# Attention with 12 heads on one Trainium2 core: the row maximum enters the second score product through a spare row, and the step lists are reordered

## The chip, the cores and the metric

One core of a Trainium2 chip. The metric is device time in microseconds of one execution of the whole program. The kernel before took 2574.82, 2577.34 and 2578.39 us in three runs, median 2577.34.

## What is computed

32 images of 3x224x224 are cut into 196 patches each and embedded to 192 numbers; 128 text rows are joined, so a batch has T = 324 tokens of D = 192 (three tiles of 108). Then follow a causal attention with rotary positions, and a block with a second attention and a mixture of 8 experts, of which each token takes 2. The change touches the second attention only:

```
qkv = (xn @ qkv_w.T + qkv_b).reshape(Bx, Nx, 3, H, hd).transpose(2, 0, 3, 1, 4)   # H = 12, hd = 16
q, k, v = (qkv[0], qkv[1], qkv[2])
attn = softmax(einsum('bhqd,bhkd->bhqk', q, k) * hd ** -0.5, axis=-1)
o = einsum('bhqk,bhkd->bqhd', attn, v)
```

## The kernel before

**Stages.** The work on a batch is split in a front (embedding, first attention, products for q, k, v of the second), a back (the second attention), a close (projection, norm, gate, places of the tokens, scatter to a buffer in DRAM) and expert tiles of 256 token rows, three a turn. A body of the loop runs the front of batch b, the back of b-1 and the close of b-2. Bodies of the list BOTH also run three expert tiles. The order is: BOTH for batches 0 and 1 (without the parts that have no batch yet), ATTEND for fronts 2 to 18 (17 bodies), BOTH for 19 to 31 (13 bodies), LAST (back of batch 31), CLOSE, and then 17 turns of expert tiles alone (TILES).

**Order by lists.** ATTEND_STEPS, BOTH_STEPS and LAST_STEPS are written out. Each engine runs its own steps in the list's order, and between engines semaphores decide. Each list has its banks of PSUM (..._BANKS): a step on TensorE waits (free) until the step that reads the bank's last contents is done, as FREED says: s is freed by mx, mt by nm, st by ex.

**The second attention, per batch.** A head has 32 partitions, so four heads fill a group g of 128; three groups. 16 rows of a head hold one copy of its 16 numbers, the other 16 a second copy; qm is the f16 part of q in the rows that the mask mq picks, QA = q - qm (L1346), KH = f16(k) (L1027), KL = k - KH (L1348).
- s (L1778, TensorE, 18 steps): the scores of two heads and one tile of queries, two matmuls QA x KH, 32 rows deep, 324 columns. The step's number p even or odd picks partitions 0 to 63 or 64 to 127.
- mx (L1356, VectorE, 18): the row maximum, written in row 0 of each head's 32 in MX, which is otherwise zero.
- mt (L1787, TensorE, 3): three transposes of MX, one group.
- nm (L1042, ScalarE, 3): NM = -MX^T / BIG, f16, from PSUM.
- st (L1801, TensorE, 18): the transposed scores of two heads and one tile of keys, as the sum of three products of two matmuls each: KH x QA, KL x QA, and big16 x NM (big16 is BIG = 32768 everywhere), which subtracts the maximum.
- ex (L1051, ScalarE, 18): the exponential; pv (L1812, TensorE): the product with v; no (L1366 to L1371, VectorE): the division by the sums.

The other steps that the text names: emb (L1657 with tokW, freed by he L1235), tr1 and tr2 (transposes, L1621 and L1622), qk1, v1, qk2, v2, W1, W2, pj, gate (chains, all L1657), s1 (L1728), p1t (L1739), X (L1851) and pos (L1839, L1841) on TensorE; qkh (L1026) and v2e (L1034, L1036) on ScalarE; rm (L1316), m1 (L1325), qkl, the steps of gt1 and pos2 (L1393 to L1440), yv (L1506) on VectorE; scat (L876), ad (L899) and gb (L887) on POOL; xin, keep, lr, lu, ld (loads and stores) on SyncE.

TensorE's steps in a body, in the order of the lists. ATTEND before:

```
s0 s1 s2 emb s3 s4 s5 s6 pj mt0 tr1 s7 st0 st1 st2 s8 qk1.0 qk1.1 s9 st3 v1 s10 st4 st5 s11 s12 s1. s13 mt1 s14 pv0
s15 s16 p1t st6 s17 pv1. st7 mt2 st8 st9 st10 tr3 st11 st12 st13 gate st14 st15 tr2 pv1 pos st16 st17 qk2.0 qk2.1
qk2.2 pv2 v2                                        (s1. and pv1. belong to the first attention)
```

BOTH before:

```
X0 emb s0 s1 W1 pj W1 s2 s3 s4 W1 s5 tr1 W2 s6 s7 W2 s8 s9 qk1.0 X1 v1 W1 s10 s11 qk1.1 mt0 W1 s12 st0 st1 W1 s1. W2
st2 st3 W2 mt1 s13 st4 s14 X2 s15 st5 p1t st6 st7 W1 s16 pv1. tr3 s17 W1 st8 st9 pv0 mt2 W1 st10 st11 gate st12 st13
pv1 W2 st14 pos tr2 st15 W2 st16 st17 qk2.0 qk2.1 pv2 v2 qk2.2
```

## Time and profile before

| | us |
|---|---|
| runs, median | 2577.34 |
| profiled execution | 2573.1 |
| its span, first to last instruction | 2571.3 |
| TensorE (PE) busy | 2368.5 |
| weight loads (PEld), beside PE | 1829.1 |
| VectorE (DVE) busy | 1657.7 |
| ScalarE (ACT) busy | 1156.4 |
| GpSimd (POOL) busy | 1042.0 |

PE is TensorE's matmuls, PEld its weight loads, SP is SyncE, which issues the transfers. Busy times leave out waits. Matmuls are pipelined, so the busy times of neighbouring groups overlap, and the sum over groups is more than the engine's. PEclk is the granted clock of TensorE as a share of 2.4 GHz; it has two levels, 1.2 and 2.4 GHz, so 0.5 is a stretch wholly at the lower. The letter L and a number name a line of the kernel.

### The profile page before, as it was taken

What the parts mean: (1) busy time and instruction counts of PE and PEld (TensorE: products, weight loads), DVE (VectorE), ACT (ScalarE), POOL (GpSimd) and SP (SyncE); (2) the same over time, 40 slices, a digit from 0 to 9 for tenths busy, and PEclk for the clock granted to TensorE, in tenths of its full rate; (3) what the DMA queues carried; (4) which work ended last, traced back from release to release, by engine and by line L of the source; (5) the groups of instructions that cost most, each with busy time, mean ns of one, the idle gap of its engine ahead of it and who ended that gap; (6) DMA issues with size and microseconds to landing.
All of it is one profiled execution on the core that took longest, in us unless ns stands there. A gap on an engine that the chain in (4) does not pass through costs nothing. (4 is left out here: it accounts for less than half of the span.)

```text
span 2571.3 us, 63751 instructions
## 1 busy us (share of the span) xinstructions
PE 2368.5 (92%) x19496; PEld 1829.1 (71%) x19496; DVE 1657.7 (64%) x4146; ACT 1156.4 (45%) x2240; POOL 1042.0 (41%) x1196
## 2 busy tenths in 40 slices
PE   5589999999999999999999999999999987999996
PEld 4456666666666666677777777777777767989886
DVE  3558888888888888867776677766677651111111
ACT  2234444344443344345555555555555643333332
POOL 2103233332333333334444444454444454565565
PEclk7669999999999999899999999999999998999998
DMA  7445222322222322533444554443344355877874
GB/s 135 142 61 111 32 36 35 49 40 32 36 33 44 47 32 32 141 68 102 115 98 106 119 117 104 97 116 91 101 110 106 87 148 183 232 225 225 239 218 132
DMA packets 182885, 268.48 MB, mean 104 GB/s; under 512 B 34085, under 2 KB 150249, under 8 KB 182825
## 3 DMA queue, kind: packets, MB, share of 16 engines
q1 hardware_dynamic: 145960, 235.45, 37.4%
q0 software_dynamic: 36864, 32.27, 7.1%
q8 instruction: 33, 0.54, 0.1%
q14 instruction: 28, 0.22, 0.0%
HBM read 217.71 MB, written 58.33 MB: 107 GB/s over the span
## 5 line engine op out<-in xcount | busy, mean ns | idle before, releaser
L1356 DVE TENSOR_REDUCE MX<-PS 108x2 f32<-108x648 f32 x576 | 455.9, 824 | 46.3 <-PE PS L1778 41.6
L1051 ACT ACTIVATE pool<-PS 108x648 f32<-108x648 f32 x576 | 386.8, 713 | 214.0 <-PE PS L1801 185.7
L899 POOL DMA_INDIRECT out<-big,tokn x192 | 304.2, 1584 | 415.7 <-DVE big L1506 234.0
L1657 PE MATMUL PS<-WB,big 128*128 128x192 f32 x2304 | 405.8, 331 | 2.5 <-ACT big L1080 2.5
L1080 ACT ACTIVATE big<-PS,WF 128x256 f32<-128x256 f32 x576 | 241.9, 473 | 350.3 <-PE PS L1657 348.3
L1657 PEld LDWEIGHTS PS<-WB,big 128*128 128x128 f32 x2304 | 374.8, 191 | 27.8 <-issue 19.1
L1657 PE MATMUL PS<-XE,WF 128*128 128x256 f16 x2880 | 358.9, 276 | 22.8 <-DMA WF<-w1p 15.0
L1657 PEld LDWEIGHTS PS<-XE,WF 128*128 128x128 f16 x2880 | 274.5, 99 | 75.9 <-issue 16.9
L876 POOL DMA_INDIRECT xbuf<-XR,DST x192 | 190.6, 993 | 238.4 <-issue 154.1
L1506 DVE SCALAR_TENSOR_TENSOR big<-PS,grow,GB 128x192 f32<-128x192 f32 x192 | 71.2, 413 | 271.6 <-POOL GB L887 152.7
L1812 PE MATMUL PS<-pool,Vp 108*32 108x324 f32 x2304 | 216.2, 518 | 0.0
L1368 DVE RECIPROCAL rsi<-rsi 128x324 f32<-128x324 f32 x96 | 209.1, 2178 | 3.3
L1778 PE MATMUL PS<-KH,QA 32*108 32x324 f16 x1152 | 155.2, 339 | 48.3 <-DVE MX L1356 11.2
L1657 PE MATMUL PS<-tokW,ximg 96*88 96x192 f32 (+1 forms) x1024 | 196.4, 352 | 3.5 <-issue 2.6
L1657 PEld LDWEIGHTS PS<-tokW,ximg 96*88 96x88 f32 (+1 forms) x1024 | 187.6, 255 | 7.9 <-issue 4.1
L1801 PE MATMUL PS<-QA,KH 32*108 32x324 f16 x1152 | 164.6, 346 | 13.1 <-DVE MX L1356 9.9
L887 POOL TENSOR_SCALAR GB<-WB,grow 128x192 f32<-128x192 f32 x192 | 163.4, 1056 | 29.0 <-DVE grow L1518 24.6
L1778 PEld LDWEIGHTS PS<-KH,QA 32*108 32x108 f16 x1152 | 58.8, 120 | 141.8 <-issue 43.2
L1042 ACT ACTIVATE NM<-PS 128x324 f16<-128x324 f32 x96 | 42.2, 439 | 244.1 <-PE PS L1787 244.1
L1801 PE MATMUL PS<-NM,big 32*108 32x324 f16 x1152 | 150.9, 311 | 0.0
L1801 PE MATMUL PS<-QA,KL 32*108 32x324 f16 x1152 | 150.8, 311 | 0.0
L1812 PEld LDWEIGHTS PS<-pool,Vp 108*32 108x32 f32 x2304 | 73.2, 124 | 99.2 <-issue 58.1
(197 smaller groups left out, 4094.8 us busy)
## 6 DMA issues: line engine op xcount, KB each, us to landing
WF<-w1p SPq DMA_DIRECT2D x96, 771.5 KB, 5.0
WB<-w2p SPq DMA_DIRECT2D x96, 672.0 KB, 6.6
ximg<-in_x SPq DMA_DIRECT2D x96, 196.0 KB, 5.4
XtR<-xbuf SPq DMA_DIRECT2D x96, 196.0 KB, 2.6
ximg<-in_x SPq DMA_DIRECT2D x96, 195.1 KB, 8.7
out<-R SPq DMA_DIRECT2D x32, 243.0 KB
w1p<-WF SPq DMA_DIRECT2D x8, 768.0 KB, 4.1
w2p<-in_L_ffn_W SPq DMA_DIRECT2D x8, 576.0 KB, 8.7
```

The costliest lines, as they stand in the source:

```text
L876: nc.gpsimd.indirect_dma_start(xbuf[:, :], bass.IndirectOffsetOnAxis(ap=DST[:, NT * k + t:NT * k + t + 1], axis=0), XR[:, t, :], None).the ...
L887: last = nc.gpsimd.tensor_scalar(GB[:, i % 2, s_, :], B2t[:, i, :], grow[:, i, s_:s_ + 1], None, ALU.mult)
L899: nc.gpsimd.indirect_dma_start(rows_out, bass.IndirectOffsetOnAxis(ap=tokn[:, i, s_:s_ + 1], axis=0), Yt[:, i, s_, :], None, bounds_check= ...
L1051: nc.scalar.activation(Pr[:, at:at + 2, :], pair(("st", p))[0:TP, :, 0:T], ACT.Exp, scale=SCALE2).then_inc(S["ex"], 1)
L1080: last = nc.scalar.activation(hid[:, i, c, :], ps[:, TILE * (c % 2):TILE * (c % 2) + TILE], ACT.Gelu, bias=WF1[:, i, 2 * HID + c:2 * HID + ...
L1356: nc.vector.tensor_reduce(MX[:, qt, g, 64 * jj:64 * jj + 64:32], pair(("s", p))[0:TP, :, 0:T], AX.X, ALU.max).then_inc(S["mx"], 1)
L1368: nc.vector.reciprocal(at, at).then_inc(S["inv"], 1)
L1506: last = nc.vector.scalar_tensor_tensor(Yt[:, i, s_, :], bank(("W2", i, 0))[:, D * s_:D * s_ + D], grow[:, i, s_:s_ + 1], GB[:, i % 2, s_, ...
L1657: last = nc.tensor.matmul(out_ap, lhsT, rhs, start=(i == 0), stop=(i == len(products) - 1))
L1778: last = nc.tensor.matmul(ps[0:TP, i, 0:T], QA[r, g, TP * qt:TP * qt + TP], KH[r, g, :], start=True, stop=True)
L1801: last = nc.tensor.matmul(ps[0:TP, i, 0:T], left[r], right[r], start=n == 0, stop=n == 2)
L1812: last = nc.tensor.matmul(ps[32 * j:32 * j + 32, 0:T], Vp[:, kt, 4 * g + j, :], Pr[:, at, :], start=kt == 0, stop=kt == NT - 1)
```

## The change

The third product of st goes. The maximum takes a row that the second product has spare: MX is now written from row 16 (HD) of each head on; BIG is added to the bias of that row of k's low part, so that KL holds BIG there (C_TOP, qmb[:, 3:6]); the mask mq now picks rows 0 to 15, so that qm is the f16 part of q there and zero in rows 16 to 31; and nm adds -MX^T / BIG to qm in place, on VectorE instead of ScalarE. st becomes KH x QA + KL x qm: two products, and KL's product with the low part of q is left out. NM and big16 go. All three lists are reordered, with their banks. What is left out of the diff are the hunks of the other lists and banks.

```diff
--- before.py
+++ after.py
@@ -59,7 +59,8 @@
 C_I = C_J + NJ
 C_LE = C_I + NTL
 C_TOK = C_LE + E * E
-C_N = C_TOK + NT
+C_TOP = C_TOK + NT
+C_N = C_TOP + 1
 
 XIN = 6 * 16
 FRONT_STEPS, BACK_STEPS = 6, 17
@@ -83,8 +84,8 @@
     SP=("xin", "text", "keep", "rows0", "rows1", "rows2", "up0", "up1", "up2", "down0", "down1", "down2"),
     PE=("emb", "tr1", "qk1", "v1", "s1", "p1t", "pv1", "tr2", "qk2", "v2", "s", "mt", "st", "pv", "pj", "tr3", "gate",
         "pos", "x_full", "w1", "o_full"),
-    ACT=("tr1h", "v1e", "e1", "p1e", "tr2h", "qkh", "v2e", "nm", "ex", "xm", "xh", "th", "x_evac", "gelu"),
-    DVE=("he", "var0", "n0", "tr1l", "rm", "m1", "rcp", "h1", "var1", "n1", "xf", "tr2l", "qkl", "fstep", "mx", "sums",
+    ACT=("tr1h", "v1e", "e1", "p1e", "tr2h", "qkh", "v2e", "ex", "xm", "xh", "th", "x_evac", "gelu"),
+    DVE=("he", "var0", "n0", "tr1l", "rm", "m1", "rcp", "h1", "var1", "n1", "xf", "tr2l", "qkl", "fstep", "mx", "nm", "sums",
          "inv", "no", "x1", "var3", "na", "n3", "logit", "hot", "tin", "gt2", "pos2", "bstep", "y_done", "gs", "gm"),
     POOL=("eps0", "is0", "rs", "eps1", "is1", "hb", "cx", "ch", "rr", "eps3", "is3", "xl", "gb"))
 
@@ -96,74 +97,74 @@
 ATTEND_STEPS = [
-    ("s", 0), ("text",), ("s", 1), ("s", 2), ("emb",), ("mx", 0), ("s", 3), ("mx", 1), ("mx", 2), ("s", 4), ("he",),
-    ("s", 5), ("mx", 3), ("st0",), ("mx", 4), ("is0",), ("s", 6), ("mx", 5), ("pj",), ("n0",), ("mt", 0), ("tr1",),
-    ("mx", 6), ("x1",), ("nm", 0), ("s", 7), ("st", 0), ("tr1h",), ("st", 1), ("mx", 7), ("st", 2), ("tr1l",),
-    ("ex", 0), ("cx",), ("s", 8), ("mx", 8), ("qk1", 0), ("ex", 1), ("rm", 0), ("qk1", 1), ("ex", 2), ("s", 9),
-    ("st", 3), ("ex", 3), ("v1",), ("rs", 0), ("s", 10), ("rm", 1), ("mx", 9), ("st", 4), ("mx", 10), ("v1e",),
-    ("st", 5), ("ex", 4), ("st3",), ("s", 11), ("ex", 5), ("rs", 1), ("s", 12), ("s1",), ("mx", 11), ("mx", 12),
-    ("s", 13), ("mt", 1), ("m1",), ("s", 14), ("is3",), ("mx", 13), ("pv", 0), ("e1",), ("mx", 14), ("s", 15),
-    ("mx", 15), ("s", 16), ("p1t",), ("nm", 1), ("mx", 16), ("st", 6), ("n3",), ("p1e",), ("s", 17), ("ex", 6),
-    ("pv1",), ("st", 7), ("ex", 7), ("mx", 17), ("xin",), ("rcp",), ("mt", 2), ("nm", 2), ("st", 8), ("h1",),
-    ("st1",), ("is1",), ("st", 9), ("ex", 8), ("st", 10), ("tr3",), ("ex", 9), ("st", 11), ("no", 0), ("ex", 10),
-    ("xm",), ("st", 12), ("ex", 11), ("st", 13), ("n1",), ("xh",), ("ex", 12), ("gate",), ("ex", 13), ("st", 14),
-    ("st", 15), ("tr2",), ("tr2h",), ("gt1",), ("rr",), ("tr2l",), ("pv", 1), ("pos",), ("ex", 14), ("st", 16),
-    ("st", 17), ("ex", 15), ("pos2",), ("ex", 16), ("qk2", 0), ("ex", 17), ("keep",), ("ch",), ("qk2", 1), ("qkh", 0),
-    ("th",), ("xl",), ("no", 1), ("qkl", 0), ("qkh", 1), ("gt2",), ("qk2", 2), ("pv", 2), ("v2",), ("qkl", 1),
-    ("hb",), ("qkh", 2), ("qkl", 2), ("xf",), ("no", 2), ("v2e",), ("scat",),
+    ("s", 0), ("text",), ("emb",), ("mx", 0), ("s", 1), ("s", 2), ("he",), ("mx", 1), ("s", 3), ("st0",), ("mx", 2),
+    ("mx", 3), ("is0",), ("s", 4), ("pj",), ("n0",), ("tr1",), ("mx", 4), ("xin",), ("tr1h",), ("x1",), ("s", 5),
+    ("mx", 5), ("rr",), ("tr1l",), ("s", 6), ("mx", 6), ("s", 7), ("mt", 0), ("nm", 0), ("qk1", 0), ("st", 0),
+    ("mx", 7), ("rm", 0), ("qk1", 1), ("rm", 1), ("s", 8), ("st", 1), ("ex", 0), ("v1",), ("s", 9), ("rs", 0),
+    ("ex", 1), ("mx", 8), ("v1e",), ("s", 10), ("s", 11), ("rs", 1), ("mx", 9), ("s", 12), ("mx", 10), ("st", 2),
+    ("s1",), ("mx", 11), ("st3",), ("st", 3), ("mx", 12), ("m1",), ("st", 4), ("ex", 2), ("s", 13), ("ex", 3),
+    ("s", 14), ("mx", 13), ("mx", 14), ("mt", 1), ("keep",), ("ex", 4), ("e1",), ("s", 15), ("nm", 1), ("st", 5),
+    ("ex", 5), ("ch",), ("s", 16), ("cx",), ("mx", 15), ("p1t",), ("mx", 16), ("is3",), ("s", 17), ("n3",), ("rcp",),
+    ("p1e",), ("st", 6), ("ex", 6), ("st", 7), ("pv1",), ("mx", 17), ("h1",), ("mt", 2), ("ex", 7), ("st", 8),
+    ("nm", 2), ("st", 9), ("pv", 0), ("tr3",), ("ex", 8), ("ex", 9), ("st1",), ("st", 10), ("xm",), ("st", 11),
+    ("ex", 10), ("xh",), ("ex", 11), ("st", 12), ("st", 13), ("gate",), ("st", 14), ("ex", 12), ("ex", 13), ("is1",),
+    ("st", 15), ("no", 0), ("n1",), ("tr2",), ("pv", 1), ("gt1",), ("tr2h",), ("xl",), ("hb",), ("pos",), ("ex", 14),
+    ("tr2l",), ("ex", 15), ("st", 16), ("th",), ("pos2",), ("st", 17), ("gt2",), ("v2",), ("ex", 16), ("qk2", 0),
+    ("ex", 17), ("no", 1), ("scat",), ("pv", 2), ("qkh", 0), ("qk2", 1), ("xf",), ("qkl", 0), ("v2e",), ("qk2", 2),
+    ("no", 2), ("qkh", 1), ("qkl", 1), ("qkh", 2), ("qkl", 2),
 ]
...
@@ -362,17 +363,16 @@
         nw = sb("nw", [128, 2], F32)
         n2 = sb("n2", [TP, 2, D], F32)
         qkb = sb("qkb", [128, 6], F32)
-        qmb = sb("qmb", [128, 3], F32)
+        qmb = sb("qmb", [128, 6], F32)
         cst = sb("cst", [128, C_N], F32)
         ident = cst[:, C_ID:C_ID + 128]
-        m64, mq = (cst[:, c:c + 1] for c in (C_M64, C_MQ))
+        m64, mq, top = (cst[:, c:c + 1] for c in (C_M64, C_MQ, C_TOP))
         rev = cst[0:TP, C_REV:C_REV + NT * E].rearrange("p (t e) -> p t e", t=NT)
         id16 = sb("id16", [128, 128], F16)
         idb = sb("idb", [TP, TP], BF16)
         maskb = sb("maskb", [TP, TP], BF16)
         U16 = sb("U16", [TP, TP], F16)
         ones16 = sb("ones16", [TP, TP], F16)
-        big16 = sb("big16", [128, TP], F16)
 
         ximg = sb("ximg", [128, GRID * IMG], F32)
         H = sb("H", [TP, NT, D], F32)
@@ -401,7 +401,6 @@
         X1 = sb("X1", [TP, NT, D], F32)
         NB = sb("NB", [TP, NT, D], F32)
         MX = sb("MX", [TP, NT, NG3, 128], F32)
-        NM = sb("NM", [128, NG3, T], F16)
         pool1 = sb("pool1", [128, 18 * T], F32)
         Pr = pool1[0:TP, :].rearrange("p (i t) -> p i t", t=T)
         tokD = pool1[0:96, 768 * 4:768 * 5].rearrange("p (s n m) -> p s n m", s=2, n=4)
@@ -777,7 +776,6 @@
             nc.gpsimd.memset(big[0:96, 2688:3456], 0.0).then_inc(pad_set, 1)
             nc.gpsimd.memset(Vp[:, :, :, :], 1.0).then_inc(pad_set, 1)
             nc.gpsimd.memset(MX[:, :, :, :], 0.0).then_inc(pad_set, 1)
-            nc.gpsimd.memset(big16[:, :], BIG).then_inc(pad_set, 1)
             nc.gpsimd.memset(zrow[:, :, :], 0.0).then_inc(zero_set, 1)
             pool.wait_ge(zero_set, 1)
             nc.gpsimd.memset(zrow[:, :, D:D + 1], NOWHERE).then_inc(zero_set, 1)
@@ -1036,11 +1034,6 @@
                 nc.scalar.activation(Vp[:, 2, :, 0:HD], ps[0:TP, 1, 0:D].rearrange("p (h d) -> p h d", h=HEADS),
                                      ACT.Copy).then_inc(S["v2e"], 1)
 
-            def nm(b, g):
-                act.wait_ge(S["mt"], due("mt", b, g + 1))
-                act.wait_ge(S["st"], due("st", b - 1, 6 * g + 6))
-                nc.scalar.activation(NM[:, g, :], bank(("mt", g))[:, 0:T], ACT.Copy, scale=-1.0 / BIG).then_inc(S["nm"], 1)
-
             def ex(b, p):
                 act.wait_ge(S["st"], due("st", b, p + 1))
                 if p >= 9:
@@ -1092,7 +1085,7 @@
                         attention_weights()
                         continue
                     if kind == "preps":
-                        act.wait_ge(pad_set, 4)
+                        act.wait_ge(pad_set, 3)
                         prep("qkv")
                         continue
                     if kind == "ready":
@@ -1116,8 +1109,6 @@
                         qkh(b, step[1])
                     elif kind == "v2e":
                         v2e(b)
-                    elif kind == "nm":
-                        nm(b, step[1])
                     elif kind == "ex":
                         ex(b, step[1])
                     elif kind == "xm":
@@ -1196,7 +1187,8 @@
 
             def query_bias():
                 dve.wait_ge(qb_in, 128)
-                nc.vector.tensor_scalar(qmb[:, :], qkb[:, 0:3], mq, None, ALU.mult).then_inc(bias_ready, 1)
+                nc.vector.tensor_scalar(qmb[:, 0:3], qkb[:, 0:3], mq, None, ALU.mult)
+                nc.vector.tensor_scalar(qmb[:, 3:6], qkb[:, 3:6], top, None, ALU.add).then_inc(bias_ready, 1)
 
             def attention_weights():
                 for i, (v, hi, lo) in enumerate(early):
@@ -1345,7 +1337,7 @@
                 ps = pair(("qk2", j))
                 nc.vector.scalar_tensor_tensor(QA[:, j, :], ps[:, 0, 0:T], qkb[:, j:j + 1], qm[:, j, :],
                                                ALU.add, ALU.subtract)
-                nc.vector.scalar_tensor_tensor(KL[:, j, :], ps[:, 1, 0:T], qkb[:, 3 + j:4 + j], KH[:, j, :],
+                nc.vector.scalar_tensor_tensor(KL[:, j, :], ps[:, 1, 0:T], qmb[:, 3 + j:4 + j], KH[:, j, :],
                                                ALU.add, ALU.subtract).then_inc(S["qkl"], 1)
 
             def mx(b, p):
@@ -1353,8 +1345,13 @@
                 dve.wait_ge(S["s"], due("s", b, p + 1))
                 if p % 6 == 0:
                     dve.wait_ge(S["mt"], due("mt", b - 1, g + 1))
-                nc.vector.tensor_reduce(MX[:, qt, g, 64 * jj:64 * jj + 64:32], pair(("s", p))[0:TP, :, 0:T], AX.X,
+                nc.vector.tensor_reduce(MX[:, qt, g, 64 * jj + HD:64 * jj + 64:32], pair(("s", p))[0:TP, :, 0:T], AX.X,
                                         ALU.max).then_inc(S["mx"], 1)
+
+            def nm(b, g):
+                dve.wait_ge(S["mt"], due("mt", b, g + 1))
+                nc.vector.scalar_tensor_tensor(qm[:, g, :], bank(("mt", g))[:, 0:T], -1.0 / BIG, qm[:, g, :],
+                                               ALU.mult, ALU.add).then_inc(S["nm"], 1)
 
             def no(b, g):
                 dve.wait_ge(S["pv"], due("pv", b, g + 1))
@@ -1570,6 +1567,8 @@
                         qkl(b, step[1])
                     elif kind == "mx":
                         mx(b, step[1])
+                    elif kind == "nm":
+                        nm(b, step[1])
                     elif kind == "no":
                         no(b, step[1])
                     elif kind == "x1":
@@ -1794,11 +1793,10 @@
                 free(pe, turn, ("st", p))
                 ps = pair(("st", p))
                 k = slice(TP * kt, TP * kt + TP)
-                for n, (left, right) in enumerate(((KH[:, g, k], QA[:, g, :]), (KL[:, g, k], QA[:, g, :]),
-                                                   (big16[:, :], NM[:, g, :]))):
+                for n, (left, right) in enumerate(((KH[:, g, k], QA[:, g, :]), (KL[:, g, k], qm[:, g, :]))):
                     for i in range(2):
                         r = slice(64 * jj + 32 * i, 64 * jj + 32 * i + 32)
-                        last = nc.tensor.matmul(ps[0:TP, i, 0:T], left[r], right[r], start=n == 0, stop=n == 2)
+                        last = nc.tensor.matmul(ps[0:TP, i, 0:T], left[r], right[r], start=n == 0, stop=n == 1)
                 last.then_inc(S["st"], 1)
 
             def pv(turn, b, g):
@@ -1887,7 +1885,7 @@
                         continue
                     if kind == "preps":
                         pe.wait_ge(act_const, 1)
-                        pe.wait_ge(pad_set, 4)
+                        pe.wait_ge(pad_set, 3)
                         pe.wait_ge(zero_set, 3)
                         pe.wait_ge(qkv_in, 16)
                         prep("qkv")
@@ -1988,7 +1986,8 @@
     p = np.arange(128)
     c[:, C_ID:C_ID + 128] = np.eye(128, dtype=np.float32)
     c[:, C_M64] = p >= 64
-    c[:, C_MQ] = p % 32 >= HD
+    c[:, C_MQ] = p % 32 < HD
+    c[:, C_TOP] = np.where(p % 32 == HD, BIG, 0.0)
     j = np.arange(RH, dtype=np.float32)
     theta = np.power(np.float32(10000.0), np.float32(-2.0) * j / np.float32(D), dtype=np.float32)
     ang = np.arange(T, dtype=np.float32)[None, :] * theta[:, None]
@@ -2007,7 +2006,7 @@
     c[:, C_J:C_J + NJ] = np.arange(NJ) * TILE
     c[:, C_I:C_I + NTL] = np.arange(NTL)
     e = np.arange(E)
-    c[0:TP, C_TOK:C_N] = np.arange(TP)[:, None] + TP * np.arange(NT)[None, :]
+    c[0:TP, C_TOK:C_TOP] = np.arange(TP)[:, None] + TP * np.arange(NT)[None, :]
     c[:, C_LE:C_TOK] = (e[None, :] <= e[:, None]).reshape(-1)
     return c
```

TensorE's steps after, in the same manner. ATTEND:

```
s0 emb s1 s2 s3 s4 pj tr1 s5 s6 s7 mt0 qk1.0 st0 qk1.1 s8 st1 v1 s9 s10 s11 s12 st2 s1. st3 st4 s13 s14 mt1 s15 st5 s16
p1t s17 st6 st7 pv1. mt2 st8 st9 pv0 tr3 st10 st11 st12 st13 gate st14 st15 tr2 pv1 pos st16 st17 v2 qk2.0 pv2 qk2.1 qk2.2
```

BOTH:

```
X0 emb W1 s0 s1 pj W1 s2 s3 s4 W1 s5 tr1 s6 s7 W2 s8 s9 W2 s10 s11 qk1.0 X1 qk1.1 W1 v1 s12 s13 W1 mt0 s14 s15 W1 st0
st1 s1. W2 st2 st3 W2 st4 st5 mt1 X2 p1t st6 st7 W1 s16 pv1. s17 tr3 W1 mt2 st8 st9 pv0 W1 st10 st11 gate st12 st13 pv1
W2 st14 tr2 st15 W2 st16 st17 qk2.0 qk2.1 pos pv2 v2 qk2.2
```

The image load xin stands 31st of 200 steps in BOTH instead of 147th, and 19th of 149 in ATTEND instead of 87th.

## Rows read from the trace of the kernel before

**Rows 1.** The page: busy time of each engine, and the span in 40 slices

```profile
PE 2368.5 (92%) x19496; PEld 1829.1 (71%) x19496; DVE 1657.7 (64%) x4146; ACT 1156.4 (45%) x2240; POOL 1042.0 (41%) x1196
...
PE   5589999999999999999999999999999987999996
```

**Rows 2.** Windows: stretch, its us, busy us by engine, PEclk, DMA share, GB/s

```profile
185.02:1053.54 868.52, 811.03 (x6848) 570.48 (x6846) 760.93 (x1810) 355.32 (x720) 290.96 (x384) 0.94 0.27 44
1113.82:1973.82 860.00, 849.99 (x7296) 657.13 (x7296) 607.26 (x1524) 484.44 (x865) 386.11 (x432) 0.98 0.47 107
...
2130.00:2571.30 441.30, 393.24 (x3067) 367.48 (x3065) 66.46 (x274) 159.15 (x357) 244.32 (x210) 0.96 0.72 208
...
1401.05:1472.88 71.83, 70.98 (x609) 54.76 (x609) 50.61 (x128) 40.26 (x72) 32.17 (x36) 0.98 0.47 107
1472.88:1543.06 70.18, 69.33 (x609) 54.27 (x610) 50.55 (x128) 40.27 (x72) 32.16 (x36) 1.00 0.47 108
...
101.77:185.02 83.25, 64.97 (x400) 41.71 (x400) 47.27 (x84) 25.34 (x47) 9.62 (x13) 0.67 0.36 83
```

**Rows 3.** Line L1235 (he), 32 instructions, one for each batch

```profile
L1235 DVE TENSOR_TENSOR H<-PS,tokb x32: 345/358/359, 27.7 to 1973.8; 108x192 f32<-108x192 f32 x32
```

**Rows 4.** Waits in 185 to 1054 us: who waited for whom, us, times, longest

```profile
PEld PS L1778 <- DVE MX L1356: 23.9, 50, 3.8
PEld PS L1801 <- DVE MX L1356: 20.9, 48, 0.6
...
DVE H L1235 <- PE PS L1657: 23.2, 16, 5.5
DVE posn L1427 <- PE PS L1841: 19.7, 16, 1.8
DVE tmp L1316 <- PE PS L1657: 14.6, 16, 0.9
```

**Rows 5.** Groups by form, whole span: count, busy us, mean ns, idle before

```profile
L1801 PE MATMUL PS<-NM,big 32*108 32x324 f16 x1152 | 150.9, 311 | 0.0
...
L1348 DVE SCALAR_TENSOR_TENSOR KL<-PS,qkb,KH 128x324 f16<-128x324 f32 x96 | 52.4, 546 | 0.0
...
L1042 ACT ACTIVATE NM<-PS 128x324 f16<-128x324 f32 x96 | 42.2, 439 | 244.1 <-PE PS L1787 244.1
```

**Rows 6.** Timeline: start us, us, engine; a lone st, a pair of st, qkl

```profile
748.58 0.34 PE L1801 MATMUL PS<-QA,KH 32*108 32x324 f16 x2
748.76 0.30 PE L1801 MATMUL PS<-QA,KL 32*108 32x324 f16 x2
748.89 0.30 PE L1801 MATMUL PS<-NM,big 32*108 32x324 f16 x2
749.12 0.50 PE L1787 MATMUL PS<-cst,MX 108*128 108x108 f32 x3
...
599.90 0.45 PE L1801 MATMUL PS<-QA,KH 32*108 32x324 f16 x4
600.08 0.41 PE L1801 MATMUL PS<-QA,KL 32*108 32x324 f16 x4
600.22 0.41 PE L1801 MATMUL PS<-NM,big 32*108 32x324 f16 x4
600.59 0.58 PE L1657 MATMUL PS<-XT,qkvWa 128*128 128x324 f16 x3
...
712.21 0.55 DVE L1346 SCALAR_TENSOR_TENSOR QA<-PS,qkb,qm 128x324 f16<-128x324 f32 x1
712.67 0.55 DVE L1348 SCALAR_TENSOR_TENSOR KL<-PS,qkb,KH 128x324 f16<-128x324 f32 x1
```

**Rows 7.** Windows of 3 us, columns as in rows 2: two BOTH bodies, an ATTEND body

```profile
1449.00:1452.00 3.00, 3.00 (x27) 0.99 (x25) 2.23 (x13) 2.97 (x5) 0.34 (x1) 0.59 0.66 272
...
1521.00:1524.00 3.00, 3.00 (x31) 2.19 (x24) 2.57 (x14) 2.97 (x5) 0.17 (x1) 1.00 0.51 212
...
758.00:761.00 3.00, 3.00 (x25) 0.99 (x24) 2.15 (x10) 1.46 (x3) 0.00 (x0) 0.50 0.00 0
```

1 line of the change is left out of this document (added), and 141 rows, old and new, of tables (ATTEND_BANKS, BOTH_BANKS, BOTH_STEPS, LAST_BANKS).

## The prediction

> **What bounds the kernel now.** I read the page first for shares, then cut the span into its stages. TensorE is busy 2368.5 us of 2571.3, VectorE 1657.7, ScalarE 1156.4 [rows 1]; the slices show three regimes. The windows by stage [rows 2] run between first additions of he (L1235), which each attention body has once [rows 3]. 185 to 1054 us holds 16 rounds of the ATTEND body, 54.28 us each: TensorE busy 811.03 of 868.52 (93.4%), VectorE 760.93 (87.6%). 1114 to 1974 holds 12 BOTH bodies, 71.67 each: TensorE 849.99 of 860.00 (98.8%), VectorE 607.26 (70.6%). Then come the rest of the last BOTH body, LAST and CLOSE, and from about 2130 the expert tiles alone, 441 us, which hold no step that the change touches. So TensorE sets the pace of BOTH by itself. In ATTEND it leads too, with VectorE close behind.
>
> Who waits for whom in ATTEND [rows 4]: TensorE's weight loads wait for the row maxima (MX L1356) before s and st, for 0.5 us at a time; all its idle time, 868.52 less 811.03 [rows 2], is 57.5 us, 3.6 a body. VectorE idles 107.6 us, 6.7 a body, and its three longest waits, all for TensorE (L1657, L1841), are 57.5 us of that, 3.6 a body; what is left, 3.1, is shorter waits and its own chains.
>
> **The change part by part.**
>
> *The third product.* 1152 matmuls out<-NM,big go, two for each of 576 st steps. Their row says 150.9 us busy [rows 5], but busy time overlaps with the neighbours and is not the price. The price is read from starts [rows 6]. A lone st begins its three products at 748.58, 748.76 and 748.89 and the next step starts at 749.12: a product of two matmuls takes one slot of 0.13 to 0.14 us. Two st steps side by side, whose heads lie in different halves of the partitions (0 to 63, 64 to 127), start their products at 599.90, 600.08 and 600.22 as fours and are through at 600.59: 0.69 us for two, against 0.54 for one. So a neighbour is almost free, and a removed product of a full pair is worth one slot for both.
> The Trainium skill (TensorE: Matmul & The Clock Gate, the section Why this matters for your kernels) says that small-K matmuls in distinct row groups run concurrently. By that rule alone, with all steps in pairs, the product is worth 9 slots a body, half of 18. The starts agree for real pairs, but the lists don't pair every step.
> So I count slots from the lists: in each unbroken run of s and st steps on TensorE, one slot for each s, three (after: two) for each st, separately for even and odd heads' halves, and the larger sum counts. ATTEND goes from 47 to 32 slots, BOTH from 45 to 31, LAST from 43 to 36. That takes in the new order as well. At 0.137 us: 2.05 us a body in ATTEND, 1.9 in BOTH, 1.0 in LAST. Bounds: 9 slots (1.2 us), if only full pairs had counted, and 18 (2.5 us), if no pair overlapped.
>
> *nm moves from ScalarE to VectorE.* ScalarE loses 96 activations of 439 ns [rows 5], 1.3 us a body. It is busy 355 of 868 us in ATTEND and 484 of 860 in BOTH [rows 2]: worth nothing by itself. VectorE gets 96 operations on 128x324, PSUM f32 with an f16 operand to f16. The nearest row is KL (L1348), the same shape, operation and kinds: 546 ns mean, 52.4 us in all. Starts inside a burst are 0.46 us apart (QA at 712.21, KL at 712.67) [rows 6]. I take 0.55, so 1.65 us a body; bounds 0.46 and 0.65, for a wait for mt at each. Being in order, VectorE stands at nm until mt's three transposes are through, and mx, m1, x1 and the others stand behind it; who waits for those is TensorE, at the next s for a free bank. The lists put steps between mt and st (qk1 in ATTEND, s and W1 in BOTH), so st itself is covered there.
> In BOTH VectorE goes from 50.6 to 52.3 us of 71.7: hidden. In ATTEND it goes from 47.6 to 49.2, while TensorE goes from 50.7 to 48.7. The two are level. Of the 3.1 us of VectorE's idle time that is no long wait I count half, 1.5, as chains that stay, so a body can hardly be under 50.7 by VectorE. TensorE needs 48.7 and some of the 3.6 us of its waits, which grow as VectorE is later in relation to it. I let 1.3 of the 2.05 us through: body 53.0. Bounds: a gain of 2.5, if all slots count and the waits stay, and a loss of 1.65, if VectorE's whole idle time stays and the new operations lengthen the body.
>
> *The small ones.* MX in row 16 of a head's 32, qm and QA with halves exchanged, BIG added to KL's bias: same instructions, same shapes, 0. NM and big16 go, one memset less on POOL at the start, one tensor_scalar on 128x3 more, both behind the input loads: 0, bounds -0.5 and 0.5. qkh still waits for the st steps of the batch before: 0. The result loses the product of the two low parts, which is no time. The other moved steps (xin, keep, lr, lu, ld on SyncE's queue, scat, ad, gb on POOL's) issue the same transfers. POOL is busy 291 of 868 us and 386 of 860, the DMA share is 0.27 and 0.47 [rows 2]; I take 0, within the ends already given. The image load xin now stands early in both bodies instead of late.
>
> *The ends.* Body 1, before 185 us, has the first back part: TensorE 64.97 us busy of 83.25 at a clock of 0.67 [rows 2]. 14 slots at half clock are 3.8 us; with so much idle time I take 2, bounds 0 and 4. LAST: 1, bounds 0 and 2. Expert tiles: 0.
>
> *Sum.* 17 ATTEND bodies (batches 2 to 18) x 1.3 = 22; 13 BOTH bodies x 1.9 = 25; 2 + 1. Together 50 us. The profiled execution took 2573.1 (span 2571.3), so 2523; the median shown is 2577.3, 4.2 above it, so **2527**. Ends: gains of 17 x 2.5 + 13 x 2.5 + 6 = 81 give 2496; 17 x 1.65 lost, 13 x 1.2 won give 2590.
>
> **The clock** is the term that no row can fix. Two BOTH bodies with the same instructions took 71.83 and 70.18 us [rows 2]. In the first, a stretch shows a granted clock of 0.59, in the other it is 1.00 at the same place [rows 7]: one stretch at 1.2 instead of 2.4 GHz costs 1.65 us. It stands behind the gate products (8 columns each) and the st steps and the pv that follow, not behind idle time: TensorE is busy 3.00 of 3.00 us there, and so it is in ATTEND (758 to 761, at 0.50). The change takes matmuls out of just this part.
> The same page of the Trainium skill (the section HAM oscillation) blames gaps in which TensorE idles for the return to the low clock. By that rule the change would cost nothing here, as it makes no long gap. The trace differs: the drops come with TensorE busy, so the rule takes no risk off the sum.
>
> **The rivals.**
> *A, VectorE takes over ATTEND.* The three nm's wait for mt and stand in front of maxima; TensorE's faster steps only wait longer. ATTEND gains nothing, BOTH its 25: 2573.1 - 28 + 4.2 = 2549. For it: 87.6% before, and the MX waits. Against: 3.6 us a body of VectorE's idle time is long waits for TensorE, twice the 1.65 added.
> *B, the slots all count.* TensorE passes on everything at the upper ends: 2496 + 4 = 2500. For it: BOTH has no slack; unequal neighbours overlap poorly. Against: ATTEND's second engine is near.
> *C, slower: more half-clock stretches.* From one more stretch in each of 30 bodies (30 x 1.65 = 50 us) the gain is gone. Two more in each ATTEND body and one in each BOTH body are 47 x 1.65 = 78 us: 2573.1 - 50 + 78 + 4.2 = 2605. For it: less work on TensorE in the part where the clock already falls. Against: the gate, pv, pos and transposes in that part stay as they are, and the bodies shorten anyhow.
> *D, the change doesn't do what it says,* because the lists let the products go where TensorE was waiting. In BOTH, with 1.2% idle, that can't be; in ATTEND it is rival A. TensorE at its old pace in BOTH too would give 2577, with next to no chance.
>
> **How the numbers follow.** The forecast with its neighbourhood (2510 to 2542) 0.50; A 0.20; B 0.15; C 0.10; D beyond A, and what lies between no gain and the worst sum, 0.05. A measurement here tells about 0.2%, 5 us, from no change. Faster: forecast, B, nearly all of A and a little of the rest, 0.85. C and the worst sum give 0.10 slower, 0.05 same. The range holds B's centre and A with a clock stretch in half of the bodies: 2494 to 2568.
>
> **What would show it.** Right: L1801 has four matmuls a step (2304, not 3456); BOTH bodies about 69.8 us with TensorE still over 97% busy; ATTEND bodies about 53 us with VectorE at 92 to 93% and TensorE near it; the new VectorE rows near 0.55 us; the expert tiles unchanged at 441. A: ATTEND stays at 54 us, and TensorE waits for L1356 more than now. B: ATTEND under 52 us. C: a mean granted clock under the present 0.94 and 0.98 in these stages. The forecast is wrong if BOTH gains under 1 us a body, or if the gain comes from the expert tiles.

## The result, and the profile after

The change makes the kernel slower: 2714.23 us, median of four runs (2710.8 to 2720.45), against 2576.08 of the kernel before in the same comparison. The ratio is 1.056 [1.0535, 1.0585]. The forecast was 2527; its range, 2494 to 2568, doesn't hold the result. The profiled execution took 2711.8 us, its span is 2710.0, 138.7 above that of before. Medians here and in the table of the experiments are over all runs of a kernel; one run of e2 and two of e5 lie more than 1.5% above that kernel's fastest, and without them the medians are 2697 and 2814 us.

The page of the kernel after: span, TensorE's busy time, and two rows of the 40 slices (compare [rows 1]; before, the digits of PEclk were 9 from the fourth slice on but for three).

```profile
span 2710.0 us, 61359 instructions
...
PE 2424.8 (89%) x18344; PEld 1839.5 (68%) x18344; DVE 1711.0 (63%) x4243; ACT 1122.5 (41%) x2144; POOL 1043.6 (39%) x1195
...
PE   4589999998999999989999999999999986999996
...
PEclk8668787788778787789999999999999998999998
```

TensorE has 1152 matmuls less and is busy 56 us longer. The digits 7 and 8 of PEclk from the fourth slice to the eighteenth, which hold the ATTEND bodies, are what is new. The windows by stage (columns as in [rows 2]) give the sizes: start, 16 ATTEND bodies, 12 BOTH bodies, the last expert tiles.

```profile
101.77:190.35 88.58, 65.44 (x374) 40.73 (x372) 47.30 (x85) 24.14 (x44) 9.93 (x13) 0.67 0.32 78
190.35:1161.56 971.21, 889.44 (x6272) 601.68 (x6270) 774.44 (x1859) 344.25 (x672) 290.09 (x384) 0.81 0.25 39
...
1225.56:2102.17 876.61, 829.46 (x6864) 641.18 (x6862) 637.63 (x1560) 466.25 (x829) 383.95 (x427) 0.97 0.46 104
2268.00:2710.00 442.00, 392.33 (x3054) 367.17 (x3054) 65.90 (x271) 158.50 (x357) 241.73 (x207) 0.96 0.72 206
```

An ATTEND body takes 971.21 / 16 = 60.70 us instead of 54.28, 102.7 us in all; a BOTH body 73.05 instead of 71.67, 16.6 us in all. The start before the first of these bodies costs 5.3 us, the ATTEND body between the two stages 3.7, and what follows the last addition of he 10.3; the expert tiles are as before (442 us). Granted clock in ATTEND: 0.81 instead of 0.94. Time at half clock is twice the missing share: 2 x 0.19 x 971.21 = 369 us after, 2 x 0.06 x 868.52 = 104 us before. The unrounded clock record of the traces says 373 and 97; further such times in this text are from that record, between the first and the last addition of he of the 16 bodies. (The texts on the runs, written before them, name the same times up to 3 us higher, as 375 and 232 for 373 and 229.)

Three rows of the groups by form (columns as in [rows 5]): the two products that are left, and nm in its new place.

```profile
L1799 PE MATMUL PS<-QA,KH 32*108 32x324 f16 x1152 | 153.8, 379 | 21.3 <-DVE Os L1368 7.0 <-ACT XM L1050 4.9 <-DVE qm L1353 3.0
L1799 PE MATMUL PS<-qm,KL 32*108 32x324 f16 x1152 | 139.8, 339 | 0.0
...
L1353 DVE SCALAR_TENSOR_TENSOR qm<-PS,qm 128x324 f16<-128x324 f32 x96 | 46.5, 484 | 4.1 <-PE PS L1786 3.9
```

The product is gone, and nm takes 484 ns, where 550 was forecast.

**Where the clock falls.** Windows of 3 us in the ATTEND body from 369.70 to 428.66, in two stretches:

```profile
387.00:390.00 3.00, 2.27 (x20) 1.33 (x17) 2.67 (x9) 1.05 (x2) 1.06 (x2) 1.00 0.00 0
390.00:393.00 3.00, 2.76 (x25) 1.47 (x23) 3.00 (x6) 2.49 (x9) 0.00 (x0) 0.96 0.00 0
393.00:396.00 3.00, 3.00 (x14) 2.39 (x12) 2.75 (x8) 1.70 (x3) 0.00 (x0) 0.50 0.00 0
...
405.00:408.00 3.00, 2.40 (x21) 2.05 (x21) 2.76 (x11) 0.68 (x2) 1.01 (x2) 0.73 0.00 0
408.00:411.00 3.00, 3.00 (x23) 1.12 (x26) 1.90 (x9) 1.46 (x3) 0.00 (x0) 0.50 0.00 0
```

And TensorE's timeline through the first fall (start, us, engine, line, operation, out<-in):

```profile
390.74 0.34 PE L1777 MATMUL PS<-KH,QA 32*108 32x324 f16 x2
391.14 0.34 PE L1799 MATMUL PS<-QA,KH 32*108 32x324 f16 x2
...
391.88 0.76 PE L1738 MATMUL PS<-cst,P 108*108 108x108 f32 x6
...
393.02 0.51 PE L1799 MATMUL PS<-QA,KH 32*108 32x324 f16 x2
393.32 0.48 PE L1799 MATMUL PS<-qm,KL 32*108 32x324 f16 x2
393.78 4.17 PE L1656 MATMUL PS<-V,P1T 108*108 108x192 f32 x12
```

From 388.35 to 393.78 TensorE runs only 32-row products (s, st) and transposes (mt, p1t), with gaps of 0.73 and 0.18 us. Inside this run, at 392.73 by the clock record, the lower level is granted and everything takes longer: a lone product's row goes from 0.34 to 0.51 us, and the twelve matmuls of pv1 behind it take 4.17 us. The second fall (406.39) stands behind the gate, as it did before [rows 7]. In the old list pv0, 24 matmuls over 108 partitions, stood inside the first of these runs; the new list has it behind mt2, st8 and st9.

The clock record of all 16 bodies shows that this body is one of four of its kind. In the other twelve the lower level comes earlier, 16 to 19 us behind the addition of he, when TensorE has run s9 to s12 and st2 and is at s1. of the first attention; that is ahead of the place that pv0 had. Of the 373 us at half clock, 27 belong to the fall at 23 us that is shown here, 174 to the earlier one, 31 to another in nine bodies (8 us behind the addition of he, behind tr1, s5 to s7 and mt0), and 140 to the one behind the gate, where the kernel before had nearly all of its 97. So the place of pv0 can explain the new falls of this kernel in part only.

Are the gaps the cause? In BOTH before, the stretches ahead of the fall of [rows 7] have none:

```profile
1443.00:1446.00 3.00, 3.00 (x39) 2.00 (x33) 1.67 (x3) 2.58 (x4) 2.77 (x6) 1.00 1.16 116
1446.00:1449.00 3.00, 3.00 (x36) 2.16 (x34) 2.93 (x7) 2.77 (x4) 3.00 (x5) 0.84 1.07 242
```

The fall itself begins at 1448.06, and the pv that the prediction counts to its causes starts only at 1448.95. Ahead of all eleven falls of these 12 bodies TensorE is busy without a gap for 6 us (by the profile, which models the ends of matmuls). So a fall needs no idle time there that the profile shows. In the last 2.5 us ahead of 1448.06 TensorE ran st and the gate's products, and before them the wide products of a W1. That thin work alone (few rows, or few columns) is enough is what this suggests; in ATTEND thin work and gaps stand together, and the runs below separate them only in part.

**Where BOTH loses.** Two waits that the trace of before doesn't have among its long ones, from the waits of 1225.56 to 2102.17, and VectorE's and POOL's timeline at the start of one body:

```profile
DVE Nrm L1262 <- POOL rsf L811: 32.3, 11, 3.0
PE PS L1777 <- DVE X L1378: 31.3, 11, 2.9
```

```profile
1736.78 0.98 POOL L874 DMA_INDIRECT xbuf<-XR,DST  x1 [0.30 <-issue]
1737.90 1.51 POOL L885 TENSOR_SCALAR GB<-WB,grow 128x192 f32<-128x192 f32 x2
...
1739.66 0.90 POOL L811 TENSOR_TENSOR rsf<-vef,cst 108x3 f32<-108x3 f32 x1
1740.68 0.96 DVE L1262 TENSOR_SCALAR Nrm<-H,mvf,rsf 108x192 f32<-108x192 f32 x3 [2.95 <-POOL rsf L811]
...
1742.52 0.34 PE L1777 MATMUL PS<-KH,QA 32*108 32x324 f16 x2 [2.86 <-DVE X L1378]
```

The new list ends a body with scat and begins the next with gb0 ahead of is0, all on POOL: scat's transfers are still being issued until 1737.8, gb0 takes 1.5 us, is0 comes behind it, and VectorE stands at n0 with x1 and the maxima behind it. TensorE waits 2.9 us for them in this body, 31.3 in 12.

### The profile page after: what moved, and what is told of

It is laid out like the page before. It is cut to its first block and busy times, and to the rows that moved or that the text cites. A ratio compares the mean times of both kernels' runs of the same rounds, so it can differ in the third digit from the quotient of the medians.

```text
span 2710.0 us, 61359 instructions
## 1 busy us (share of the span) xinstructions
PE 2424.8 (89%) x18344; PEld 1839.5 (68%) x18344; DVE 1711.0 (63%) x4243; ACT 1122.5 (41%) x2144; POOL 1043.6 (39%) x1195
## 5 line engine op out<-in xcount | busy, mean ns | idle before, releaser
L1656 PE MATMUL PS<-WB,big 128*128 128x192 f32 x2304 | 412.6, 335 | 3.5 <-ACT big L1073 3.5
L1656 PEld LDWEIGHTS PS<-WB,big 128*128 128x128 f32 x2304 | 381.1, 194 | 25.9 <-issue 16.1
L1777 PE MATMUL PS<-KH,QA 32*108 32x324 f16 x1152 | 168.2, 363 | 79.5 <-DVE X L1378 33.9
L1810 PE MATMUL PS<-pool,Vp 108*32 108x324 f32 x2304 | 209.6, 504 | 1.7 <-ACT pool L1044 1.7
L885 POOL TENSOR_SCALAR GB<-WB,grow 128x192 f32<-128x192 f32 x192 | 170.5, 1130 | 76.0 <-DVE grow L1515 74.4
L1799 PE MATMUL PS<-QA,KH 32*108 32x324 f16 x1152 | 153.8, 379 | 21.3 <-DVE Os L1368 7.0
L833 POOL TENSOR_TENSOR tmp<-tmp 96x324 f32<-96x324 f32 x64 | 55.4, 866 | 274.4 <-DVE tmp L1308 274.4
L816 POOL TENSOR_TENSOR vef<-mvf,cst 108x3 f32<-108x3 f32 x32 | 6.8, 212 | 353.1 <-DVE mvf L1236 353.1
L1799 PE MATMUL PS<-qm,KL 32*108 32x324 f16 x1152 | 139.8, 339 | 0.0
```

Of the source, the lines that this page charges most:

```text
L885: last = nc.gpsimd.tensor_scalar(GB[:, i % 2, s_, :], B2t[:, i, :], grow[:, i, s_:s_ + 1], None, ALU.mult)
L1656: last = nc.tensor.matmul(out_ap, lhsT, rhs, start=(i == 0), stop=(i == len(products) - 1))
L1777: last = nc.tensor.matmul(ps[0:TP, i, 0:T], QA[r, g, TP * qt:TP * qt + TP], KH[r, g, :], start=True, stop=True)
L1799: last = nc.tensor.matmul(ps[0:TP, i, 0:T], left[r], right[r], start=n == 0, stop=n == 1)
L1810: last = nc.tensor.matmul(ps[32 * j:32 * j + 32, 0:T], Vp[:, kt, 4 * g + j, :], Pr[:, at, :], start=kt == 0, stop=kt == NT - 1)
```

## The experiments

Times are medians; ratios are to the kernel before, measured beside it on the same chip, with the 95% interval. The median of the kernel before was 2576 us beside after, 2579 beside e1 to e4, 2585 beside e5 to e8, 2582 beside e9 and e10, 2589 beside e11 and e12, and 2592 beside e13 to e16. So between these groups ratios are to be compared, not times, and a body's mean carries the same uncertainty, up to 0.6%. "Body" is the mean of the 16 ATTEND and the 12 BOTH bodies, "half" the time at half clock in the 16 ATTEND bodies.

| kernel | us | ratio | ATTEND body | half | BOTH body |
|---|---|---|---|---|---|
| before | 2576 | 1 | 54.28 | 97 | 71.67 |
| after | 2714 | 1.056 [1.0535, 1.0585] | 60.70 | 373 | 73.05 |
| e1 content, old lists | 2649 | 1.0267 [1.0235, 1.0299] | 58.72 | 229 | 71.74 |
| e2 old content, new lists | 2700 | 1.0468 [1.0442, 1.0494] | 58.38 | 227 | 74.97 |
| e3 after, third product of zeros | 2690 | 1.0445 [1.0424, 1.0467] | 57.84 | 201 | 74.26 |
| e4 after, nm on ScalarE | 2716 | 1.0551 [1.0522, 1.0579] | 60.08 | 336 | 74.56 |
| e5 after, wide filler | 2839 | 1.0983 [1.0925, 1.104] | 65.41 | 189 | 73.77 |
| e6 after, thin filler | 2780 | 1.0761 [1.0739, 1.0783] | 64.52 | 324 | 72.46 |
| e7 before, 9 wide at the gate | 2587 | 1.0007 [0.9989, 1.0025] | 54.93 | 34 | 71.74 |
| e8 after, gb0 behind n0 | 2712 | 1.0494 [1.0462, 1.0526] | 61.09 | 305 | 72.30 |
| e9 e1, third product of zeros | 2648 | 1.0261 [1.0235, 1.0287] | 58.27 | 185 | 71.64 |
| e10 before, 3 wide at the gate | 2558 | 0.9914 [0.9894, 0.9934] | 53.65 | 44 | 71.66 |
| e11 two products, nm on ScalarE | 2682 | 1.0355 [1.0323, 1.0387] | 60.22 | 246 | 71.69 |
| e12 e11, 3 wide at the gate | 2645 | 1.0212 [1.0187, 1.0236] | 58.93 | 192 | 71.40 |
| e13 after, pv0 earlier | 2744 | 1.0569 [1.0516, 1.0621] | 62.37 | 257 | 73.08 |
| e14 after, 3 wide at the gate | 2738 | 1.0551 [1.0519, 1.0583] | 62.26 | 373 | 72.96 |
| e15 e13 and e14 | 2745 | 1.0592 [1.0555, 1.0629] | 62.59 | 281 | 73.35 |
| e16 e1, 3 wide at the gate | 2675 | 1.0343 [1.0291, 1.0395] | 59.20 | 208 | 71.62 |

**Content and lists apart (e1, e2).** e1 is the kernel after with the three lists and the banks of before; e2 is the kernel before with those of after. The head of e1's diff against after:

```diff
 ATTEND_STEPS = [
-    ("s", 0), ("text",), ("emb",), ("mx", 0), ("s", 1), ("s", 2), ("he",), ("mx", 1), ("s", 3), ("st0",), ("mx", 2),
+    ("s", 0), ("text",), ("s", 1), ("s", 2), ("emb",), ("mx", 0), ("s", 3), ("mx", 1), ("mx", 2), ("s", 4), ("he",),
...
```

> The change's two products and nm on VectorE, in the lists and banks of the kernel before. Theory L (the order of the lists makes the clock fall more often): the ATTEND body stays near 54.3 us or gains up to 2, half-clock time between 180 and 1110 us stays near 113 us, total 2530 to 2570. Rival W (it is the missing work of the third product that lets the clock fall, wherever it stood): total above 2640, half-clock time there above 250 us. Rival V (nm on VectorE holds up the chain, the clock follows): above 2600, with VectorE waiting for L1786 and TensorE for VectorE at st.

> The new lists and banks with the old three products and nm on ScalarE. Theory L: slow by itself, above 2640, half-clock time in ATTEND above 250 us. Rival W: near the kernel before, 2560 to 2600, with the ATTEND body at 54 to 56 us. Rival V: the same as W.

Each half loses alone, 70 and 121 us, and together 138, less than the sum. Theory L fell with e1, and rivals W and V, both of which had e2 near the kernel before, fell with e2; what each said of the other run came out in part only (for e1 V's waits did show, and 229 us at half clock is under W's 250; for e2 227 us is under L's 250). The windows of e2, of ATTEND and of BOTH:

```profile
189.19:1123.26 934.07, 857.17 (x6848) 599.21 (x6846) 759.70 (x1810) 364.36 (x720) 290.55 (x384) 0.88 0.26 41
1186.30:2085.97 899.67, 850.17 (x7296) 658.01 (x7294) 628.68 (x1525) 478.87 (x865) 386.15 (x427) 0.97 0.45 102
```

In BOTH the two can be read one by one: the lists cost 3.3 us a body (71.67 to 74.97; the wait behind POOL above is 2.6 to 2.9 of it in the kernel after), the content on these lists gives 1.9 back (74.97 to 73.05), just the forecast size; on the old lists it gives nothing (71.74). In ATTEND both lower the clock. The windows of e1, of ATTEND and of BOTH, and rows of its waits in ATTEND:

```profile
184.47:1123.94 939.47, 836.51 (x6272) 574.43 (x6270) 778.43 (x1858) 343.69 (x672) 291.09 (x384) 0.88 0.25 41
1187.43:2048.36 860.93, 831.54 (x6864) 634.58 (x6864) 621.03 (x1561) 469.66 (x829) 386.57 (x432) 0.98 0.47 106
```

```profile
DVE qm L1353 <- PE PS L1786: 23.4, 16, 3.3
...
PE PS L1799 <- DVE H L1331: 19.4, 16, 1.2
...
PE PS L1777 <- DVE qm L1353: 11.6, 16, 0.7
PE PS L1799 <- DVE qm L1353: 11.4, 16, 0.8
```

In BOTH TensorE is idle 860.93 - 831.54 = 29.4 us where it was idle 10.0: what the slots give becomes waits. In ATTEND VectorE stands at nm for the transposes, and TensorE waits behind it at s and st (L1331 is h1, which stands right behind the last nm on VectorE). These three waits of TensorE are 42.4 us, 2.65 a body, more than the 2.05 that the slots were to give.

**The missing product back (e3, e9).** A third product with zeros, which adds nothing to the sum, on the new lists (e3) and on the old (e9).

```diff
-((KH[:, g, k], QA[:, g, :]), (KL[:, g, k], qm[:, g, :]))
+((KH[:, g, k], QA[:, g, :]), (KL[:, g, k], qm[:, g, :]), (KL[:, g, k], zed[:, :]))
```

> The kernel after with a third product KL x zeros in each st, which adds nothing to the scores and waits for nothing new. Theory L: as slow as the kernel after or slower by its 15 to 18 slots, 2710 to 2760. Rival W: the clock comes back, 2560 to 2620, so more work is less time. Rival V: 2710 to 2760.

> Old lists, the change's content (nm on VectorE, maximum in the second product), and a third product KL x zeros in each st: against the kernel before only nm's engine and its place differ, against the content on old lists only the third product is back. Theory W alone: half-clock time in ATTEND back from 232 us to 95 to 120, body 54 to 55, total 2565 to 2595. Rival G (on the old lists it is the gaps that nm on VectorE opens ahead of st and s that let the clock fall, not the missing work): half-clock time stays above 180 us, body 58 or more, total above 2640. Both in part: between.

On the new lists 1152 more matmuls make the kernel 24 us faster (30 us by the ratios): half-clock time goes from 373 to 201 us. That lies between the theories, none of which it fits: W wanted 2620 at most, L and V 2710 at least. On the old lists they change nothing (2649, 2648), and rival G comes out in all its signs. e9 does as many matmuls as the kernel before, and only nm's engine and place (and the operands of the third product) differ; it takes 66 us more and stands 185 us at half clock instead of 97:

```profile
183.38:1115.68 932.30, 844.51 (x6848) 599.27 (x6846) 773.75 (x1858) 344.84 (x672) 291.41 (x384) 0.90 0.24 41
```

So on the old lists nm on VectorE costs by itself nearly all that the whole content costs. TensorE waits there as in e1, 40.8 us for nm and for the h1 behind it, and is idle 87.8 us instead of 57.5. The bodies of e3 are of two kinds by turns, all of the same instructions:

```profile
357.66:412.80 55.14, 50.63 (x430) 35.33 (x428) 48.11 (x115) 21.56 (x42) 18.16 (x24) 0.94 0.25 37
412.80:473.71 60.91, 56.56 (x430) 39.42 (x428) 48.20 (x115) 21.55 (x42) 18.14 (x24) 0.83 0.20 34
```

TensorE is busy 5.9 us longer in the second at the same idle time, 4.4 to 4.5 us: the whole difference is the clock. At half clock it spends 6.8 and 20.5 us, so one us there costs 0.42 us.

**Who does nm (e4, e11, e12).** In e4 nm goes back to ScalarE, which writes -MX^T / BIG to a tile that nothing reads: the maximum isn't subtracted, and the exponent's scale is divided by 64 so that it stays finite. e11 computes all of it without that: old lists, two products, and mt itself adds qm, by one 128-row matmul per group, so that ScalarE can write the sum. e12 adds e10's filler to it.

```diff
 # e4, on ScalarE
+nc.scalar.activation(NM[:, g, :], bank(("mt", g))[:, 0:T], ACT.Copy, scale=-1.0 / BIG)
 # e11, in mt on TensorE, and on ScalarE; idn is -BIG on the diagonal
+nc.tensor.matmul(ps[:, 0:T], idn[:, :], qm[:, g, :], start=True, stop=False)
+nc.scalar.activation(qm[:, g, :], bank(("mt", g))[:, 0:T], ACT.Copy, scale=-1.0 / BIG)
```

> The kernel after with nm back on ScalarE into NM, which no product reads: the maximum is not subtracted, and the exponent's scale is cut to a 64th. VectorE has its old load. Rival V: the loss goes, below 2620. Theories L and W: within 20 us of the kernel after, 2690 to 2720.

> Old lists; the change's two products and layout, but nm stays on ScalarE: mt adds to its transposes one 128-row product of qm with -32768 times the identity in the same bank, and nm writes -1/32768 of the bank over qm. Against the kernel before 18 narrow products go, three wide ones come, VectorE has its old load. Theory G (on the old lists the content's loss is nm on VectorE): no gaps ahead of st, BOTH body 69.5 to 70.5 us, ATTEND 52.5 to 54.5, half-clock time in ATTEND under 130 us, total 2535 to 2570. Rival W (missing work of the third product lets the clock fall): half-clock time above 200 us, ATTEND 56 or more, total above 2600.

> The kernel above with the three wide matmuls ahead of the gate chains of ATTEND bodies, which gained 24 us on the kernel before. If the two gains add: 2515 to 2545, the best of all. If the clock falls elsewhere now: no better than the kernel above.

e4 is as slow as after: with the new lists nm's engine is not the cause, as L and W said and V didn't. e11 has no wait for VectorE's nm and still loses 93 us: G falls here, and W's signs all come (246 us at half clock, a body of 60.22, 2682 us). So on the old lists the loss comes with nm on VectorE and all products (e9), and it comes with nm on ScalarE and two products (e11); neither is needed for it. e11 isn't clean, though: its mt has three 128-row matmuls more, and its transposes add to them. Two bodies of e11, one behind the other:

```profile
419.88:475.18 55.30, 50.21 (x406) 35.75 (x404) 47.33 (x113) 22.35 (x45) 18.20 (x24) 0.94 0.25 37
475.18:542.68 67.50, 58.70 (x406) 39.57 (x404) 47.61 (x113) 22.35 (x45) 18.22 (x24) 0.80 0.20 30
```

12.2 us apart with the same instructions; 8.5 us of it is longer busy time, 3.7 are waits that come with it. With e12's filler half-clock time goes from 246 to 192 us and 37 us come back, more than the 24 that it gave on the kernel before, though far from the 2515 to 2545 that were named if the gains add.

**Wide or thin (e5, e6).** One matmul of zeros more behind each s and st of ATTEND, 36 a body, over 128 rows in e5 and over 32 in e6; it adds nothing to the sums.

```diff
+if turn.plan is ATTEND:
+    r = slice(0, 128)                          # e6: slice(64 * jj + 32, 64 * jj + 64)
+    last = nc.tensor.matmul(ps[0:TP, 1, 0:T], zed[r, :], qkvWa[r, 0, 0:T], start=False, stop=True)
```

> The kernel after, and behind each s and each st of ATTEND bodies one more matmul of 324 columns over all 128 rows, zeros times a weight tile, added to the second bank: 36 slots, 4.9 us of new TensorE work a body, nothing waits for more. Theory W (the clock falls because stretches of 32-row products and transposes keep too few rows of the array at work): half-clock time in ATTEND falls from 23.5 us a body to under 8, the body from 60.7 to 53 to 57 us, total 2590 to 2660. Rival I (the clock falls for TensorE's idle gaps, or for the lists as such): half-clock time stays, the body is 60.7 + 4.9, total 2760 to 2800.

> The same, but each filler has 32 rows instead of 128, in the same row group as the step's second head: the same number of instructions and columns, a quarter of the rows. Theory W: the half-clock time stays above 15 us a body, the body 60 to 65 us, total at least 60 us above the wide filler's. Rival I or a rival by which any instruction counts alike: within 20 us of the wide filler.

```profile
186.52:1233.01 1046.49, 984.88 (x6852) 638.23 (x6852) 782.45 (x1859) 349.10 (x672) 290.82 (x384) 0.91 0.23 36
```

```profile
188.39:1220.68 1032.29, 919.93 (x6848) 630.84 (x6847) 779.35 (x1858) 341.37 (x672) 290.15 (x384) 0.84 0.23 37
```

The same number of matmuls: the wide ones (first fence, e5) bring half-clock time from 373 to 189 us, the thin ones (second fence, e6) to 324. So it goes with the rows more than with the number of matmuls. But neither is free: both kernels are slower than after, and no time came back; W had e5 at 2590 to 2660 and e6 at least 60 us above it, and e6 is below it. Bodies of e5 with 3.4 us at half clock take 61.0 to 62.4 us, one of e8 with as much (below) 54.7: the 36 wide fillers cost 6.3 us or more, 0.18 each at the least. Idle time fell too in e5 (61.6 us against 81.8) and rose in e6 (112.4), so the two causes aren't wholly apart here.

**Wide work at the gate (e7, e10).** The kernel before with 128-row matmuls of 324 columns ahead of each of the gate's three chains, nine a body in e7, three in e10. They write columns of the gate's bank that nothing reads.

```diff
 for t in range(NT):
     c = slice(TP * t, TP * t + TP)
+    if turn.plan is ATTEND:
+        for _ in range(1):                     # e7: range(3)
+            nc.tensor.matmul(ps[0:TP, 64:64 + T], id16[:, 0:TP], qkvWa[:, 0, 0:T], start=True, stop=True)
```

> The kernel before, and ahead of each of the three gate chains of an ATTEND body three 128-row matmuls of 324 columns into unused columns of gate's bank: 9 slots, 1.2 us. Theory W: the half-clock stretch behind the gate (6.2 us a body, worth 3 us) goes or shrinks; ATTEND body 52.3 to 53.5 us against 54.3, total 2545 to 2565. Rival I: body 55.5, total 2595 to 2600.

> The kernel before with one 128-row matmul of 324 columns ahead of each gate chain of an ATTEND body, three in place of the nine of the run above. If the clock needs only a little more work there: half-clock time in ATTEND under 60 us at a third of the cost, body 53.3 to 54.0, total 10 to 20 us below the kernel before. If it needs all nine: half-clock time stays near 99 us, and the body is longer by 0.4 to 0.8 us, total 5 to 15 us above.

The windows of ATTEND in e7 (first fence) and in e10:

```profile
182.09:1060.98 878.89, 806.62 (x6992) 581.89 (x6990) 758.45 (x1811) 355.78 (x720) 291.28 (x384) 0.98 0.26 43
```

```profile
180.93:1039.27 858.34, 794.35 (x6896) 564.78 (x6894) 760.27 (x1810) 355.81 (x720) 291.69 (x384) 0.97 0.27 45
```

Three are the better trade: clock 0.97 instead of 0.94, TensorE busy 794.35 us instead of 811.03 [rows 2] with 48 more matmuls, and 2557.72 us, 0.9914 [0.9894, 0.9934] of before. It is the fastest version of the study. Nine raise the clock to 0.98, with 34 us at half clock, as expected, but cost as much as that gives: 2587 us, where 2545 to 2565 were expected.

**POOL's order in BOTH (e8).** The kernel after with gb0 behind n0 instead of ahead of s0.

```diff
-    ("X", 0), ("text",), ("xe", 0), ("emb",), ("gm", 0), ("W1", 0, 0), ("he",), ("gb", 0), ("s", 0), ("s", 1),
-    ("st0",), ("pj",), ("mx", 0), ("mx", 1), ("ge", 0, 0), ("is0",), ("n0",), ("W1", 0, 1), ("x1",), ("s", 2),
+    ("X", 0), ("text",), ("xe", 0), ("emb",), ("gm", 0), ("W1", 0, 0), ("he",), ("s", 0), ("s", 1),
+    ("st0",), ("pj",), ("mx", 0), ("mx", 1), ("ge", 0, 0), ("is0",), ("n0",), ("gb", 0), ("W1", 0, 1), ("x1",), ("s", 2),
```

> The kernel after with one step of the BOTH list moved: gb of tile 0 stands behind n0 instead of ahead of s 0. Theory P (in BOTH the new list makes POOL, still busy with scat and then gb, late for is0, so that n0 and x1 on VectorE and the next s on TensorE wait): BOTH body shorter by 1.0 to 1.6 us, total 13 to 21 us below the kernel after. Rival (the wait for x1 has another cause): no difference.

TensorE's longest wait for X falls from 2.9 to 1.4 us, and a BOTH body from 73.05 to 72.30 us, 9 us in 12, less than the 1.0 to 1.6 us a body that were expected:

```profile
PE PS L1777 <- DVE X L1378: 13.0, 11, 1.4
```

So gb0 is part of that wait; that scat's issues are the rest is argued from the timeline above, not tried. The ratio fell from 1.056 to 1.0494, but the profiled spans are level (2709.8 and 2710.0), since the 16 ATTEND bodies, which the edit doesn't touch, went from 60.70 to 61.09, and the one behind them from 64.0 to 67.1. They show how far the clock moves them with the waits that come with it (one of the two shortest, and the longest):

```profile
442.15:496.90 54.75, 48.14 (x394) 32.53 (x392) 48.16 (x115) 21.29 (x42) 18.18 (x24) 0.97 0.26 38
...
251.21:319.34 68.13, 59.40 (x394) 40.06 (x392) 48.39 (x115) 21.44 (x42) 18.16 (x24) 0.75 0.20 30
```

The rows stand here in the order of their length. 13.4 us lie between them, at 3.4 and 34.1 us of half clock: 0.44 us for one us.

**Two of the places at which after's clock falls (e13 to e16).** e13 is after with pv0 back in the first run of thin steps, behind s17; e14 is after with e10's three matmuls at the gate; e15 has both; e16 is e1 with those three.

```diff
-    ("ex", 5), ("ch",), ("s", 16), ("cx",), ("mx", 15), ("p1t",), ("mx", 16), ("is3",), ("s", 17), ("n3",), ("rcp",),
+    ("ex", 5), ("ch",), ("s", 16), ("cx",), ("mx", 15), ("p1t",), ("mx", 16), ("is3",), ("s", 17), ("pv", 0), ("n3",), ("rcp",),
...
-    ("nm", 2), ("st", 9), ("pv", 0), ("tr3",), ("ex", 8), ("ex", 9), ("st1",), ("st", 10), ("xm",), ("st", 11),
+    ("nm", 2), ("st", 9), ("tr3",), ("ex", 8), ("ex", 9), ("st1",), ("st", 10), ("xm",), ("st", 11),
```

> The kernel after, with one step moved in the ATTEND list on TensorE: pv0 (matmuls over 108 partitions) goes from behind mt2, st8, st9 to behind s17, into the stretch of s, mt, st, s, p1t behind which the granted clock of after falls first in a body (0.50 at 393 to 399 us). Theory 1, what matters is wide work between the thin steps: the first fall goes in most ATTEND bodies, half-clock time in the 16 bodies goes from 375 us to under 250, the ATTEND body from 60.7 to 57.5 us or less, about 2660 us in all. Theory 2, the fall doesn't depend on this place (another step is late, or the clock falls whenever the body is this short): half-clock time stays over 320 us and the time within 2700 to 2725.

> The kernel after with three added 128-row, 324-column matmuls at the gate of each ATTEND body (their results go to columns of the gate bank that nothing reads), the edit that took 24 us off the kernel before. Theory 1: it guards the second stretch only (the gate), so half-clock time goes from 375 to between 200 and 300 us and the time to 2660 to 2690. Theory 2, the same edit is worth as much as before or less, because the bodies only settle in another pattern: half-clock time over 320 us, 2700 or more.

> Both edits: pv0 earlier and three 128-row matmuls at the gate in ATTEND. Theory 1, the clock is the whole of the ATTEND loss and these two stretches are where it falls: half-clock time under 120 us, the ATTEND body 54 us or less, 2590 to 2620 us in all (what is left over the kernel before is the reordered lists' wait in BOTH and the start). Theory 2, more than these stretches count: half-clock time 200 us or more, time over 2640.

> The content of the change on the old lists (two products, maximum merged on VectorE), with three added 128-row matmuls at the gate of each ATTEND body. Theory 1, the 70 us that the content cost on the old lists are clock: half-clock time in ATTEND from 232 us to under 120, the body from 58.7 to about 54.5, time 2580 to 2600. Theory 2, they are waits of TensorE for VectorE, and the clock follows them: half-clock time stays over 180, time 2635 or more.

The theory that the two guarded places bring the time back fell: e14, e15 and e16 came out as the second theory of each said. e13 is split: half-clock time falls from 373 to 257 us, nearly as the first said, but the time doesn't fall (ratio 1.0569, after 1.056), as the second said. With pv0 moved, the falls 8 us behind the addition of he go from nine bodies to two, and the long ones at 16 to 19 us from twelve to three; the other thirteen bodies keep 6.8 us at 24.5 us and 6.8 us behind the gate. But the moved pv0 waits for the read of its bank by a maximum:

```profile
PE PS L1810 <- DVE MX L1348: 44.9, 16, 3.0
```

2.8 us a body, and the rest of the body shifts with it. Twelve of its bodies take 61.4 to 61.5 us each, with 13.7 us at half clock each:

```profile
565.02:626.43 61.41, 51.19 (x394) 34.08 (x392) 47.82 (x116) 21.25 (x42) 18.09 (x24) 0.89 0.23 34
626.43:687.87 61.44, 51.19 (x394) 34.04 (x392) 47.81 (x116) 21.25 (x42) 18.09 (x24) 0.89 0.22 34
```

TensorE is idle 10.2 us in such a body, twice as long as in one of after, and stands less at half clock: the falls don't follow idle time alone. In e14 the filler at the gate changed nothing (373 us; ratio 1.0551 against 1.056), and in e16 it changed a body that varied (57 to 64 us) into one of 58.0 us, thirteen times, with half-clock time at 208 instead of 229 us; the ratio rose from 1.0267 to 1.0343. What the filler gave before (24 us) and in e12 (37 us) it doesn't give here. So guarding a place doesn't tell by itself what comes of it: the falls at other places move or stay, and the bodies settle in a pattern that repeats, a good or a bad one. That a fall makes what follows late and so moves the next thin run is the likely link; no run shows it alone.

## Why the prediction was wrong

**The step that failed is the term of the clock.** The text named it "the term that no row can fix", saw the falls in the part from which matmuls were to be taken, had rival C for it, and then left it out of the sum with a chance of 0.10. C's size was also too small: two stretches more in each ATTEND body and 78 us; measured are 276 us more at half clock in 16 bodies, 17.2 us in each, and at 0.35 to 0.44 us for one us (after's own bodies, 58.8 us with 17.1 and 62.4 with 27.3, and e8's) this is 97 to 121 us of the 102.7.

The sum for an ATTEND body closes with it. Slots: -2.05, as forecast. Idle time of TensorE: 81.8 us instead of 57.5, +1.5. Clock: 276 x 0.4 / 16 = +6.9 (0.4 taken between the two). Together +6.4; measured +6.42. For a BOTH body: slots -1.9; idle time 47.2 us in 12 instead of 10.0 in 12, +3.1; clock 48 against 38 us, +0.3; together +1.5; measured +1.4. In BOTH, e2 against after measures the slots together with nm's move: 1.9. In ATTEND the -2.05 is not measured: with 0.35 to 0.43 for the clock the sum leaves room for 1.1 to 2.5. Bodies with near the same time at half clock give a rough size: with 20.5 us TensorE is busy 56.5 us in e3 and 55.7 in e2, which have the third product, and 54.6 in after (between its bodies with 17.1 and 23.9 us, 53.6 and 55.6). So the product was worth 1.1 to 1.9 us of busy time there, under the 2.05 of the forecast.

**C's argument against itself failed.** "The gate, pv, pos and transposes in that part stay as they are, and the bodies shorten anyhow." They stayed, but new falls came in other places: 232 of the 373 us don't lie behind the gate. The list moved pv0 out of the first thin run, and in e2, with the same list, 15 of the 16 bodies fall there, 6.8 us each; in after four do, and twelve fall earlier, for which no run isolates a cause. I counted slots in the new lists and didn't read them for the runs between wide steps. e2 shows what that was worth: the lists alone, with all three products, bring half-clock time from 97 to 227 us. The content alone brings it to 229 (e1), nm on VectorE with all products to 185 (e9), and two products with nm on ScalarE, and mt changed for it, to 246 (e11).

**Moved steps on POOL at 0 was wrong** in BOTH: the new order costs 3.3 us a body, most of it the wait behind scat at the end of one body and gb0 at the head of the next (e8 shows 0.75 us for gb0). I had taken POOL's busy share, 386 of 860 us, as cover. It says nothing about where in the body POOL is busy: is0 stands behind both, n0 behind is0, and TensorE behind n0's engine.

**The gain of the slots in BOTH** (1.9) was right on the new lists and zero on the old, where waits took it. In e1 most of them are for VectorE; but e11, with nm on ScalarE, has a BOTH body of 71.69 us too, so what takes the gain there stays open. I had BOTH as bound by TensorE and let all of it through for either.

**nm** was forecast at 0.55 us, measured 0.484. Rival A was wrong as a whole: VectorE is busy 774 of 971 us in ATTEND, 80%, less than before. But a wait for nm did appear where the lists weren't made for it, 2.65 us a body in e1, over the 1.65 that I had as the bound.

**The rule on idle gaps.** The Trainium skill (TensorE: Matmul & The Clock Gate, the section HAM oscillation) puts the return to the low clock down to gaps. In BOTH before the clock falls after stretches with TensorE busy 3.00 of 3.00, and twelve of e13's bodies have twice the idle time of after's and less time at half clock. So the measurement decides against gaps as the only cause; e9, where the added gaps come with 88 us more at half clock and the work is the same, speaks for them as one of the causes. The prediction was right not to rest on that rule, and then didn't draw the conclusion: if work and not idle time lets the clock fall, the edits to the work had to be priced by it.

**What stays open.** Which share of ATTEND's loss belongs to the fewer products, to nm's place and to the order: each lowers the clock when it comes alone (246 us at half clock in e11, 185 in e9, 227 in e2, from 97), and they don't add up to the 276 us by which the whole change raises it. Also the 10.3 us behind the last addition of he; e2, with 17.7 us there, points to the new lists for a smaller part of it (e1, on the old lists, has 7.2 already), but the list LAST wasn't tried by itself. And thin work wasn't separated from short gaps in ATTEND by a run that changes one alone.

## What to carry to other kernels

Where TensorE's clock already falls once in a body, cost a change by what it does to the runs of thin matmuls (few rows, few columns, transposes) between wide ones, before counting the matmuls that it saves: here 1152 fewer, in new lists, left the engine busy 56 us longer. Look for both directions: three wide matmuls that compute nothing, at the place of the fall, took 24 us off this kernel; but try it on the final kernel, since on the others it gave 37 us once (e12), nothing twice (e14, and e15 against e13), and cost time once (e16). And read a queue's order across the seam between two bodies, since a low busy share doesn't tell that the last step of one and the first of the next stand ahead of the step that everyone needs.

## What was unexpected

Bodies with the same instructions settle in patterns: 61.4 us twelve times (e13), 58.0 thirteen times (e16), 55.1 and 60.9 by turns (e3), 55.3 and, by turns with it, 67.5 or 64.3 (e11). In these the time at half clock repeats with them to 0.1 us. This suggests that the clock and the length of a body set each other, and a small edit elsewhere can change the pattern: e8 edited BOTH only, and ATTEND bodies (all but the last of the 16) went from a spread of 58.7 to 62.4 us to one of 54.7 to 68.1.

More work can take less time: e3 has 1152 matmuls more than after and takes 24 us less (ratio 1.0445 against 1.056), e10 has 51 more than before and takes 24 us less too.
